# Feed-forward layer norms on ScalarE instead of VectorE, a spread table for the token sums, and one weight cast moved behind a norm

## The reference, cut to what matters

```python
x = x + _L0_attn_ref(_layernorm(x), ...)
x = x + _L0_xattn_ref(_layernorm(x), ctx_1024, ctx_1024, ...)
x = x + _L0_ffn_ref(_layernorm(x), w_gate, w_up, w_down)

def _layernorm(x, axis=-1, eps=1e-05):
    m = jnp.mean(x, axis=axis, keepdims=True)
    v = jnp.var(x, axis=axis, keepdims=True)
    return (x - m) / jnp.sqrt(v + eps)

def _L0_ffn_ref(x, w_gate, w_up, w_down):        # weights: int32 / 127
    gate = jnp.einsum('bsd,hd->bsh', x, wg)      # 512 -> 1536
    up = jnp.einsum('bsd,hd->bsh', x, wu)
    h = jax.nn.silu(gate) * up
    return jnp.einsum('bsh,dh->bsd', h, wd)      # 1536 -> 512
```

## Time and profile before

| what | value |
| --- | --- |
| median of three runs | 1193.99 us (1193.2 to 1194.45) |
| the profiled execution's own time | 1193.53 us |
| its span in the trace | 1191.5 us |
| TensorE busy | 1151.1 us, 97% of the span |
| VectorE busy | 872.4 us, 73% |
| ScalarE busy | 548.3 us, 46% |
| GpSimd busy | 431.7 us, 36% |
| mean granted TensorE clock | 0.991 |

### The profile page before, as it was taken

The page is one execution under the profiler, slowest core; times in us unless marked ns, Lnnn a source line. Parts: engine busy times, 40 slices in busy tenths (PEclk is TensorE's granted clock), DMA queues, the critical chain, the costliest instruction groups (busy, mean ns, idle before and its releaser), DMA issues.

```text
span 1191.5 us, 17227 instructions
## 1 busy us (share of the span) xinstructions
PE 1151.1 (97%) x6432; PEld 935.4 (79%) x6432; DVE 872.4 (73%) x1352; ACT 548.3 (46%) x862; POOL 431.7 (36%) x383
## 2 busy tenths in 40 slices
PE   7999999999989999999999997999999998999998
PEld 6777778777767888888888885878778887888886
DVE  6666675684684657876687798875899878888775
ACT  5354454455364345554445444554444445444431
POOL 1255765665753300200020034022445842444431
PEclk9899999999989999999999998999999999999999
DMA  8001010200133434333334332223311111511101
GB/s 292 9 28 45 10 63 1 80 37 23 50 111 130 166 132 142 115 101 142 121 125 149 116 121 73 80 80 123 124 54 54 54 53 63 170 53 53 53 18 71
DMA packets 53570, 103.88 MB, mean 87 GB/s; under 512 B 4848, under 2 KB 17136, under 8 KB 52464
## 3 DMA queue, kind: packets, MB, share of 16 engines
q1 hardware_dynamic: 53488, 102.78, 25.8%
HBM read 85.99 MB, written 16.78 MB: 86 GB/s over the span
## 4 chain that ended last, share of the span: by engine, by line
PE 81%; DVE 9%; ACT 4%; issue 3%; POOL 3%; ACTq 0%; DVEq 0%; POOLq 0%
PE work L189 15%; PE work L190 14%; PE work L191 14%; PE score L189 4%; PE score L190 4%; PE score L191 4%; PE score L2523 4%; PE score L2524 4%; PE score L2525 4%; PE score L1165 2%; PE work L2523 2%; PE work L2525 2%; PE work L2524 2%; PE score L1179 1%; PE work L1092 1%
## 5 line engine op out<-in xcount | busy, mean ns | idle before, releaser
L508 POOL TENSOR_TENSOR probs<-probs,band 128x544 f32<-128x544 f32 (+1 forms) x64 | 92.4, 1444 | 87.3 <-ACT probs L639 87.0
L2196 POOL TENSOR_TENSOR hid<-fg,hid 128x512 fp32r<-128x512 f32 x48 | 84.4, 1778 | 106.5 <-ACT hid L2263 106.5
L189 PE MATMUL score<-pt_h,cn_h 128*128 128x512 f32 x256 | 101.8, 398 | 9.5 <-DVE pt_l L1672 5.9
L1512 POOL TENSOR_TENSOR xr<-xr,bv_row 128x512 f32<-128x512 f32 x16 | 27.3, 1731 | 228.1 <-DMA xr<-x_scratch 228.1
L190 PE MATMUL score<-pt_l,cn_h 128*128 128x512 f32 x256 | 100.6, 393 | 0.0
L191 PE MATMUL score<-pt_h,cn_l 128*128 128x512 f32 x256 | 100.5, 393 | 0.0
L189 PE MATMUL work<-x_q_h,ct_h 128*128 128x512 f32 x256 | 100.3, 392 | 0.0
L191 PE MATMUL work<-x_q_h,ct_l 128*128 128x512 f32 x256 | 99.7, 389 | 0.0
L190 PE MATMUL work<-x_q_l,ct_h 128*128 128x512 f32 x256 | 99.7, 389 | 0.0
L2402 DVE SCALAR_TENSOR_TENSOR fx<-work,fx 128x512 f32<-128x512 f32 x96 | 65.7, 685 | 40.2 <-PE work L191 40.2
L189 PE MATMUL work<-wqkv_h,xt_h 128*128 128x512 f32 (+1 forms) x256 | 94.0, 367 | 0.0
(11 more groups left out here) (254 smaller groups left out, 3176.1 us busy)
## 6 DMA issues: line engine op xcount, KB each, us to landing
ct_raw<-in_ctx_t SPq DMA_DIRECT2D x32, 512.0 KB, 4.6
cn_raw<-in_ctx_n SPq DMA_DIRECT2D x32, 512.0 KB, 3.8
w_stage<-in_wg_t SPq DMA_DIRECT2D x12, 512.0 KB, 4.1
w_stage<-in_wu_t SPq DMA_DIRECT2D x12, 512.0 KB, 3.8
wd_raw<-in_wd_t SPq DMA_DIRECT2D x12, 512.0 KB, 3.7
x_in<-in_x SPq DMA_DIRECT2D x16, 256.0 KB, 2.8
xs<-in_x SPq DMA_DIRECT2D x4, 1024.0 KB, 5.2
x_scratch<-xs SPq DMA_DIRECT2D x4, 1024.0 KB, 4.7
```

The lines of the kernel that those rows point to most:

```text
L189: pe.matmul(out, hi_s, hi_m, start=first, stop=False)
L508: PL.tensor_tensor(probs[:, n % 2, :, 0:w], probs[:, n % 2, :, 0:w], band[:, c0:c0 + w].unsqueeze(1).to_broadcast([P, HPG, w]), ALU.mult). ...
L2196: PL.tensor_tensor(hid[:, q, 1, :], g[:, q, :], hid[:, q, 0, :].bitcast(F32), ALU.subtract).then_inc(hidl_done, 1)
```

## The change

It has three parts.

First, the sixteen norms of the feed-forward layer are activations on ScalarE (`act_norm`) instead of `tensor_scalar` on VectorE. Their bias is a new column `nb`, written for all eight tiles by one small VectorE instruction (`dve_shifts`). For the first half that instruction stands at the end of slot 40, right behind the statistics, and the norms stand in slots 41 to 44 of ScalarE, behind the copy of the scores. For the second half it stands where the VectorE norms stood, and the norms stand on ScalarE at it = 3: four behind the second `act_hidden`, four behind the last.

Second, `TOKENS_AT` goes from slots 45, 48, 52, 55 to 45, 49, 53, 57.

Third, `part_hi(WO)` stands behind `norm1` in unit 3 of sequence 0 instead of ahead of it.

```diff
-                    if not s and n in (0, 3):
-                        part_hi(WO if n else VALUES)
+                    if not s and n == 0:
+                        part_hi(VALUES)
                     if n in (3, 4, 5, 6) and more:
                         norm1(s + 1, n - 3)
+                    if not s and n == 3:
+                        part_hi(WO)
...
-    TOKENS_AT = {45: 0, 48: 1, 52: 2, 55: 3}
+    TOKENS_AT = {45: 0, 49: 1, 53: 2, 57: 3}
...
             if j + LEAD < NSL:
                 act_scores(act, j + LEAD)
+            if 41 <= j < 45:
+                ffn.act_norm(act, 2 * (j - 41))
+                ffn.act_norm(act, 2 * (j - 41) + 1)
...
             if j in (36, 40):
                 ffn.dve_stats(dve, (j - 36) // 4)
-            if 41 <= j < 45:
-                ffn.dve_norm(dve, 2 * (j - 41))
-                ffn.dve_norm(dve, 2 * (j - 41) + 1)
+            if j == 40:
+                ffn.dve_shifts(dve)
...
+    def act_norm(act, s, t):
+        act.wait_ge(nb_done, s + 1)
+        A.activation(xn[:, t, :], xn[:, t, :], ACT.Identity, bias=nb[:, t:t + 1], scale=rstd[:, t:t + 1])\
+            .then_inc(xn_done, 1)
...
             act_hidden(act, it, 1)
+            if it == HB - 3:
+                for t in range(ST):
+                    act_norm(act, 1, t)
...
             act_hidden(act, it, 2)
...
             act_hidden(act, it, 3)
+            if it == HB - 3:
+                for t in range(ST, TH):
+                    act_norm(act, 1, t)
...
-    def dve_norm(dve, s, t):
+    def dve_shifts(dve, s):
+
         dve.wait_ge(rstd_done, 2 * s + 2)
-        V.tensor_scalar(xn[:, t, :], xn[:, t, :], mv[:, t, 0:1], rstd[:, t:t + 1], ALU.subtract, ALU.mult)\
-            .then_inc(xn_done, 1)
+        V.scalar_tensor_tensor(nb[:], mv[:, :, 0], -1.0, rstd[:], ALU.mult, ALU.mult).then_inc(nb_done, 1)
...
             if it == HB - 3:
-                for t in range(TH):
-                    dve_norm(dve, 1, t)
+                dve_shifts(dve, 1)
```

More of the change, by code:

```diff
@@ L1893, in __init__ @@
             programs[n] for n in ("pool_roots", "pool_tokens", "pool_weights", "pool_rest"))
[L1894 to L1897, removed]
+        self.act_float, self.act_norm, self.act_weights, self.act_turned, self.act_rest = (
+            programs[n] for n in ("act_float", "act_norm", "act_weights", "act_turned", "act_rest"))
+        self.dve_stats, self.dve_shifts, self.dve_weights, self.dve_turned, self.dve_rest = (
+            programs[n] for n in ("dve_stats", "dve_shifts", "dve_weights", "dve_turned", "dve_rest"))
         self.pe_turn, self.pe_rest = programs["pe_turn"], programs["pe_rest"]
@@ L1991, in ffn_programs @@
     rstd = small.put("frstd", [P, TH])
+    nb = small.put("fnb", [P, TH])
     U2, U3, U4, C22 = (u[:, i, :] for i in range(4))
@@ L2002, in ffn_programs @@
     rstd_done = sem("frstd_done")
+    nb_done = sem("fnb_done")
     xn_done = sem("fxn_done")
@@ L2604, in ffn_programs @@
                        act_turned=lambda act, j: act_turned(act, 0, j), act_rest=act_rest,
-                       dve_stats=lambda dve, h: dve_stats(dve, 0, h), dve_norm=lambda dve, t: dve_norm(dve, 0, t),
+                       dve_stats=lambda dve, h: dve_stats(dve, 0, h), dve_shifts=lambda dve: dve_shifts(dve, 0),
+                       act_norm=lambda act, t: act_norm(act, 0, t),
                        dve_weights=dve_weights, dve_turned=lambda dve, j: dve_turned(dve, 0, j), dve_rest=dve_rest,
```

## The result

| what | before | after |
| --- | --- | --- |
| median of the runs | 1193.8 us (1193.2 to 1194.45, 4 runs) | 1202.0 us (1201.19 to 1202.29, 4 runs) |
| ratio to before, 95% interval | | 1.0068, 1.005 to 1.0085 |
| the profiled execution's own time, its span | 1193.53, 1191.5 | 1202.24, 1200.2 |
| TensorE, VectorE, ScalarE busy | 1151.1, 872.4, 548.3 us | 1154.4, 865.0, 560.4 us |

The changed kernel is slower by 0.68%, 8.2 us (6.0 to 10.1). So about 2.1 us were lost in slots 40 to 60 and 4.9 us at the start of it = 4.

A forecast was written before the change was run, and what follows sets the result against it. TensorE, busy 97% of the span, was taken as the bound, with slots 40 to 48 bound by VectorE. 1.8 + 0 + 0 + 3.4 + 1.5 = 6.7 us on 1193.53 gave 1200.2, median-adjusted by 0.46 to 1200.7; range 1195.5 to 1205.0.

The forecast's parts named there:

- First half, plus 1.8: Slots 40 to 45: waits 2.3, 2.8 and 0.7 us come back on VectorE, norms leaving save 4.0: plus 1.8 us.
- Extra collisions with the residuals, nothing: Slot 41: by the skill's port-sharing rule, GpSimd's residual adds would slow three VectorE steps, 3.2 us; counted as nothing.
- Token table, 0: GpSimd's token sums: same instructions and order, held only by the last norm; the new table spreads and costs nothing, 0 us.
- weight cast, 0: Self-attention: TensorE's waits of 1.21 us for the norm and 0.33 for ScalarE's copy become one of 1.54, 0 us.
- Second half, plus 3.4 and 1.5: Start of it = 4: norms delay ScalarE's copy of p0, TensorE waits 3.4 us more, then loses 1.5 to the clock.
- The clock: Behind the 3.4 us gap at the start of it = 4: low clock level expected, plus 1.5 us, between 0 and 2.3.
- The relief reaches TensorE: Rival, slots 41 to 44: the norms' VectorE time becomes TensorE time, minus 2.8 us, total 1194.6 us; chance 0.10.
- no gap at p2: Rival, start of it = 4: copy of p0 still in time, second half costs nothing, total 1195.8 us; chance 0.07.

The follow-up runs named there:

- six late norms: Changed kernel with two of the second half's norms ahead of the first hidden cast of it = 3 and six behind the last: 1202.69 us.
- the run of cast and table: Kernel before with only the output weights' cast behind the norm and the new table of slots for GpSimd's token sums: 1193.59 us.
- the kernel before with held token sums: Kernel before, norms left on VectorE, each GpSimd token sum waiting for VectorE's subtraction of slot 49, 51, 54 or 57: 1189.01 us.
- the changed kernel with held token sums: Changed kernel, each GpSimd token sum waiting for VectorE's subtraction of slot 49, 51, 54 or 57: 1195.91 us.
- all three mends: Changed kernel with second half's norms in ScalarE's idle time of it = 3, first half's fnb and norms one slot later, token sums held back: 1187.79 us.
- the run with later norms: Changed kernel with fnb at the end of slot 41 and the first half's norms in slots 42 to 45 on ScalarE: 1198.71 us.

## Why the prediction was right, point by point

The forecast was 1200.7 us in a range of 1195.5 to 1205.0, slower with 0.79. It came to 1202.0: right in sign, in size and in its two places. By its terms:

- *First half, plus 1.8.* Side by side, VectorE's `x_mx` of slot 44 starts at 722.09 instead of 719.76, 2.33 us later, 0.5 of which it brought along: 1.8 us. The terms hold one by one: the wait for the roots is 2.12 us (2.00 was priced), four waits for the exponential are 0.70 each, those for `cn_h` 0.25 and 0.26 (0.35). One was mis-sized: `fnb`, priced as `fve` at 0.17 us, took 1.25, because a residual addition ran beside it; the first norm pair, counted at 0.99 us although it was 2.18 long, made up for that. What the sum did not hold is the meeting of the shift with the token sums. The prediction had these sums start when the last norm ends, "near 722.96" (722.47 in the trace), and did not see that this norm had stood behind the shift and no longer does. In the trace this costs little net, since the steps of slots 46 and 47 paid before what the shift pays now: TensorE's waits grow by 1.1 us, the clock takes 0.6 us more. Alone, the part measures plus 3.1 (1.7 to 4.4).
- *Extra collisions with the residuals, nothing.* Before, that stretch slowed a norm pair and three steps of slot 42; now it slows `fnb`, `pt_l`, `cn_l` and `x_maxima` of slot 41. The loss changed its owners more than its size: each step's time less its usual one adds up to 4.4 us before and 3.8 now. The 3.2 us that the rule would have added did not come.
- *Token table, 0, and weight cast, 0.* The table holds: GpSimd's four sums still follow each other directly. The cast holds in its waits, the merged one is 1.73 us where 1.54 was priced, but not in the clock, which the prediction did not ask about here: the low level stands behind this wait in six traces of eight and behind the two shorter ones in none of five. Alone, table and cast measure plus 1.0 us, with nothing in the interval (minus 0.5 to 2.4), so the time does not settle what that costs.
- *Second half, plus 3.4 and 1.5.* 3.22 us of waiting and 1.6 of clock in the trace, plus 5.5 us (3.5 to 7.4) alone. The working holds: from the second cast to the copy it counted 7.35 us (924.80 to 932.15), and the trace has 7.23 (927.25 to 934.48) where it was 3.56 before (924.80 to 928.36). What it leaves unsaid is that the norms do not cost alike. Of the 3.7 us by which they put the copy off, the four behind the last cast make 2.8 and the four between the casts 0.8, because the last two casts had waited for VectorE there. That was overlooked in the expectation for six late norms, which counted all norms in full, and that run shows it: a norm between the casts is nearly free, one behind the last costs its 0.72 us.
- *The clock.* The size came out, the reason did not, so the size is in part luck. The prediction took 3.4 us as "nearer to the one that cost speed (3.58) than to the one that did not (2.49)". The length of a wait alone does not decide: a wait of 2.49 us was followed by the low level in the run of cast and table, one of 1.49 us (733.53, its first matmul 0.77 us long) in the kernel before with held token sums, and one of 3.22 us was not in the changed kernel with held token sums. The term should have been a chance of losing 1.6 us, not a loss read off a length.
- *The rivals.* "The relief reaches TensorE" did not come, because the exponential's wait of 0.70 stands in each of slots 42 to 45, which no longer have a norm on VectorE; "no gap at p2" did not come either. With all three mends the kernel takes 1187.8 us, but the kernel before with held token sums takes 1189.0, so a relief of 1.2 us at most is left, and the intervals do not show it.

## What to carry to other kernels

Work that is moved to an idle engine must be given the place where that engine idles, not only its share of busy time: eight norms cost 5.5 us ahead of a copy that TensorE waits for and nothing that shows 10 us earlier. An instruction that needs another engine's result belongs a slot behind the instruction that starts it. And a table of slots holds nothing back on an engine with nothing else to do; if GpSimd's work shall stay out of a tight stretch of VectorE, it needs a wait for VectorE's progress, and here that one line gained 4.7 us, while the norms on ScalarE, with every mend, added nothing to it that the intervals show.

## What the runs showed of the hardware

In these rows, VectorE's steps that read only SBUF do not share with GpSimd; they queue behind it. In the run with held token sums, `x_acc` starts 0.57 us after a token sum and ends 0.55 us after its end, 2.40 us for 0.69 us of work, while the next step takes its usual 0.68. So the price of a collision is about what is left of GpSimd's instruction, whatever the size of VectorE's: 128x4 elements took 2.07 us instead of 0.16, and `x_spread`, a copy with one input, 2.51 instead of 0.43. `x_s`, which reads one input from PSUM, was not held up. The Trainium skill, "SBUF — State Buffer", section "SBUF: two separate sides", calls the pair of ports that the two engines share an exclusive lock for the whole of an instruction, and "not a bandwidth split"; the rows agree.

It works the other way round as well. GpSimd's two roots take 2.01 us while VectorE waits for them and 3.14 us while VectorE works on beside them over SBUF (the run with later norms). The 2.00 us of the earlier trace rows were taken beside a busy VectorE too, but its steps there (905.60 to 907.39) each read one input from PSUM.

The clock's fall has no fixed place. Runs of one and the same kernel scatter by some 4 us here (1191.6 to 1195.5 in ten runs of cast and table), and the traces show a likely source of it: waits that agree to 0.01 us with the low level behind them in one trace and not in another (the merged wait of self-attention in six of eight). The times go with the clock: of the twenty runs of the kernel before beside that of cast and table, the seven with a mean granted clock of 0.993 took 1190.9 to 1192.2 us, the nine with 0.991 took 1193.2 to 1194.4, and the four with 0.989 took 1194.9 to 1195.6. What decides whether the clock falls behind a given wait stays open.
